# An adaptive layer-norm block on one core: the second batch's residual is stored ahead, and its gated tiles are added in the output by transfers from GpSimd

## The chip, the cores and the metric

One core of one Trainium2 chip runs the whole program. The metric is the device time of one execution in microseconds. A time given for a kernel is the median of several executions; a trace is one execution taken with the hardware profiler, and has its own time and its own span (from the first to the last recorded instruction).

## The reference

Two batches of 512 tokens with 512 features, all in float32. A condition vector `c` per batch gives six rows of modulation (shift, scale and gate for each of two sublayers).

```
mod = silu(c) @ wmod                      # per batch: sa, ca, ga, sb, cb, gb
ga, gb = sign * max(abs(.), 0.25)
h = layernorm(x) * (1 + ca) + sa
x = x + ga * (h @ (weight * blockmask).T)
h = layernorm(x) * (1 + cb) + sb
g = silu((h @ Wg.T) * ag) * ((h @ Wu.T) * au)      # 1376 inner features
out = x + gb * ((g @ Wd.T) * ad)
```

What matters here is the last line: the final result is the residual `x` after the first sublayer, plus a product that is scaled by a gate row per batch.

## The kernel before, in words

The tokens are held as eight tiles of 128 tokens by 512 features, `xt[:, n, :]`, four of each batch (`TT` is 4, `n = b * TT + t`). The kernel writes each engine's program out by hand, in one order, and ties the engines together with semaphores; there is no scheduler.

The first part loads the inputs, makes the modulation columns, normalises, and multiplies by the masked attention weight. GpSimd's `add_to_x` (L310) adds the gated product to `xt` and raises `x1_ok`: from then on `xt` holds the residual of the second sublayer, for `n` = 0 to 7. These tiles are normalised again (L497, for the second batch into `modw`), and for the second batch SyncE's sixteen block copies (L266) and VectorE's transposes (L504) bring them into the form that the matmuls want.

The feed-forward part runs over `STEPS` = 22 steps, 11 chunks of inner features for each batch. In a step TensorE makes the gate and up products (L793), ScalarE the silu, VectorE their product in two parts, and two steps later TensorE multiplies by the down weight into four accumulators, banks 4 to 7, one for each token tile (L863). For the second batch's last tile the accumulator is in two halves of 256 columns, in bank 7 and bank 3 (L849). `down_last` runs the last four steps' down products tile by tile, so that the accumulators are finished one after the other: tile 0, 1, 2, then the two halves of tile 3. `acc_mm` and `half_mm` say so.

Two rows of gates, one per batch, are broadcast over all partitions into `gates`: ScalarE copies them into `grow`, SyncE writes them to `gate_line` in memory (L270) and loads them back to all partitions (L273).

The end of a batch: VectorE's `gate_ffn(b, t)` (L619) multiplies an accumulator by the gate row, into `xn[:, t, :]`, and raises `acc_read`. For the first batch GpSimd adds it to `xt` (L329) and SyncE stores the tile (L278). For the second batch VectorE does both: after each `gate_ffn(1, t)` it waits for it and adds `xn` to `xt` (L685), then the same for the two halves of tile 3 (L691, L694). ScalarE's queue issues the stores of the second batch as `out_last` counts up, three whole tiles (L451) and two halves (L456). SyncE's last wait is for all nine stores.

SyncE's queue in order of its program: the loads, the sixteen block copies, the wait for `grow_ok`, the two writes of `gate_line`, the broadcast load, the four stores of the first batch, the last wait. GpSimd's queue: constants, `add_to_x`, the reciprocal deviations, and last the four additions of the first batch.

Of the kernel before, what the change touches and what calls it, by code (L numbers as in the profile page):

```python
# [25 lines left out]
ALU = mybir.AluOpType  # L26
# [3 lines left out]
P = 128  # L30
D = 512
KT = D // P
NB = 2
TT = 4
# [10 lines left out]
BY_POOL = TT  # L45
# [6 lines left out]
HALF = D // 2  # L52
# [14 lines left out]
def adaln_block(nc, x, att_w, att_mask, cond, mod_ln1, mod_ln2, mod_gate, w_gu, w_gu_tail, w_down,  # L67
                scales, scales_tail, down_scale, out):
    with ExitStack() as ctx:
# [3 lines left out]
        def sem(name):  # L73
            return ctx.enter_context(nc.semaphore(name))


        xt = sb("xt", [P, NB * TT, D])
        xn = sb("xn", [P, TT, D])
# [70 lines left out]
        d_ffn = [sem(f"d_ffn{c}") for c in range(C)]  # L149
        d_small = sem("d_small")  # L150
        d_out = sem("d_out")

        zeroed = sem("zeroed")
        tail_zero = sem("tail_zero")
# [36 lines left out]
        x1_ok = sem("x1_ok")  # L191
# [15 lines left out]
        acc_mm = sem("acc_mm")  # L207
        acc_read = sem("acc_read")
        out_ok = sem("out_ok")
        out_last = sem("out_last")  # L210
        half_mm = sem("half_mm")
        half_read = sem("half_read")

# [10 lines left out]
        @block.sync  # L224
        def _(sp):
            for t in range(TT):
                sp.dma_start(xt[:, t, :], x[t * P:(t + 1) * P, :]).then_inc(d_x[t], 16)  # L227

            def load_att(k):
                sp.dma_start(maskt[:, k, :], att_mask[k * P:(k + 1) * P, :]).then_inc(d_mask[k], 16)  # L230

                sp.dma_start(modw[:, k // 2, 2 * (k % 2):2 * (k % 2) + 2, :], mod_ln1[k])\
                  .then_inc(d_ln1[k], 16)
                sp.dma_start(awork[:, k, :], att_w[k * P:(k + 1) * P, :]).then_inc(d_att[k], 16)

            def load_x(t):
                sp.dma_start(xt[:, t, :], x[t * P:(t + 1) * P, :]).then_inc(d_x[t], 16)

            for k in range(KT):
                load_att(k)  # L240
            for t in range(TT, NB * TT):
                load_x(t)
            sp.dma_start(modw[:, 2, :, :], mod_gate[0]).then_inc(d_gate[0], 16)
            sp.wait_ge(rows_done, 2)
            sp.dma_start(modw[:, 0, :, :], mod_ln2[0]).then_inc(d_ln2[0], 16)
            for c in range(C):
                if c == H1_CHUNK:
                    sp.wait_ge(att_done, NB * TT)
                if c == 1:
                    sp.wait_ge(rows_done, 4)  # L250
                    sp.dma_start(modw[:, 1, :, :], mod_ln2[1]).then_inc(d_ln2[1], 16)
                    sp.wait_ge(rows_done, KT + 1)
                    sp.dma_start(modw[:, 2, :, :], mod_gate[1]).then_inc(d_gate[1], 16)
                if c < C - 1:
                    sp.dma_start(wffn[:, c, 0:2 * D], w_gu[c]).then_inc(d_ffn[c], 16)
                    sp.dma_start(raw_d(c), w_down[c * P:(c + 1) * P, :]).then_inc(d_ffn[c], 16)
                else:
                    sp.wait_ge(tail_zero, 1)
                    sp.dma_start(wffn[:, c, 0:2 * D].rearrange("p (n i) -> p n i", i=P)[:, :, 0:FT],
                                 w_gu_tail).then_inc(d_ffn[c], 16)  # L260
                    sp.dma_start(wffn[0:FT, c, 2 * D:3 * D], w_down[c * P:F, :])\
                      .then_inc(d_ffn[c], 16)
            sp.wait_ge(xn_ok, 4 * TT)
            for j in range(P // BLK):
                for i in range(P // BLK):
                    sp.dma_start(modw[BLK * j:BLK * (j + 1), 1, :, i * P:(i + 1) * P],  # L266
                                 modw[BLK * i:BLK * (i + 1), 0, :, j * P:(j + 1) * P]).then_inc(d_blocks[j], 16)
            sp.wait_ge(grow_ok, 1)
            for b in range(NB):
                sp.dma_start(gate_line[b], grow[b * KT:(b + 1) * KT, :]).then_inc(d_line, 16)  # L270
            sp.wait_ge(d_line, 16 * NB)
            sp.wait_ge(msum_ok, KT)
            sp.dma_start(gates[:, NB:2 * NB, :].rearrange("p b n -> p (b n)"),  # L273
                         gate_line.rearrange("b k i -> (b k i)").partition_broadcast(P))\
              .then_inc(d_gates, 16)
            for n in range(BY_POOL):
                sp.wait_ge(out_ok, n + 1)
                sp.dma_start(out[n * P:(n + 1) * P, :], xt[:, n, :]).then_inc(d_out, 16)  # L278
            sp.wait_ge(d_out, 16 * (NB * TT + 1))


        @block.gpsimd
        def _(pool):
            pool.memset(ident[:, :], 0.0).then_inc(ident_z, 1)
            pool.memset(mhalf[:, :], -0.5).then_inc(ident_z, 1)
            pool.wait_ge(ident_z, 2)
            pool.affine_select(out=ident[:, :], in_=ident[:, :], compare_op=ALU.not_equal, fill=1.0,  # L287
                               base=0, pattern=[[-1, P]], channel_multiplier=1).then_inc(ident_ok, 1)

            def inverse_deviation(q, half):  # L290

                two = slice(2 * half, 2 * half + 2)
                pool.wait_ge(stats_ok, TT * q + 2 * half + 2)
                pool.tensor_scalar(veps[:, q, two], mv[:, q, two, 1], EPS, None, ALU.add)\
                    .then_inc(veps_ok, 1)
                pool.wait_ge(veps_ok, 2 * q + half + 1)
                pool.tensor_tensor(rstd[:, q, two], veps[:, q, two], mhalf[:, 0:2], ALU.pow)\  # L297
                    .then_inc(rstd_ok, 1)

            def mask_weights(k):  # L300
                pool.wait_ge(d_att[k], 16)
                pool.wait_ge(keep_ok, k + 1)
                w = awork[:, k, :].rearrange("p (b i) -> p b i", i=BLK)
                pool.tensor_tensor(w, w, keep[:, k, :].unsqueeze(2).to_broadcast([P, NBLK, BLK]),
                                   ALU.mult).then_inc(masked, 1)

            def add_to_x(b, t):
                n = b * TT + t
                pool.wait_ge(att_read, n + 1)
                pool.tensor_tensor(xt[:, n, :], xt[:, n, :], xn[:, t, :], ALU.add).then_inc(x1_ok, 1)  # L310

            inverse_deviation(0, 0)
            inverse_deviation(0, 1)
            for k in range(KT):
                mask_weights(k)
            inverse_deviation(1, 0)
            inverse_deviation(1, 1)
            for b in range(NB):
                for t in range(TT):
                    add_to_x(b, t)  # L320
                inverse_deviation(2 + b, 0)
                inverse_deviation(2 + b, 1)
                if b == 0:

                    pool.wait_ge(att_done, NB * TT)
                    pool.memset(wffn[:, C - 1, :], 0.0).then_inc(tail_zero, 1)
            for n in range(BY_POOL):
                pool.wait_ge(acc_read, n + 1)
                pool.tensor_tensor(xt[:, n, :], xt[:, n, :], xn[:, n % TT, :], ALU.add)\  # L329
                    .then_inc(out_ok, 1)  # L330


        @block.scalar
        def _(act):
# [92 lines left out]
            for s in range(STEPS):  # L427
# [18 lines left out]
                    act.activation(grow[:, :], bank[3][0:KT * NB, 0:P], ACT.Copy).then_inc(grow_ok, 1)  # L446
                if 6 <= s < 10:
                    modulate(6 + s)
            for n in range(BY_POOL, NB * TT - 1):
                act.wait_ge(out_last, n - BY_POOL + 1)  # L450
                act.dma_start(out[n * P:(n + 1) * P, :], xt[:, n, :]).then_inc(d_out, 16)  # L451
            n = NB * TT - 1
            for i in range(2):
                cols = slice(i * HALF, (i + 1) * HALF)
                act.wait_ge(out_last, n - BY_POOL + 1 + i)
                act.dma_start(out[n * P:(n + 1) * P, cols], xt[:, n, cols]).then_inc(d_out, 16)  # L456


        @block.vector
        def _(dve):  # L460
# [218 lines left out]
                    for t in range(TT):  # L679
                        gate_ffn(0, t)  # L680
            for t in range(TT - 1):
                n = TT + t
                gate_ffn(1, t)
                dve.wait_ge(acc_read, n + 1)
                dve.tensor_tensor(xt[:, n, :], xt[:, n, :], xn[:, t, :], ALU.add)\  # L685
                   .then_inc(out_last, 1)
            n = NB * TT - 1
            for i, src in enumerate((bank[7], bank[3])):
                cols = slice(i * HALF, (i + 1) * HALF)
                dve.wait_ge(half_mm, i + 1)  # L690
                dve.scalar_tensor_tensor(xn[:, TT - 1, cols], src[:, cols], 2.0, gates[:, 3, cols],  # L691
                                         ALU.mult, ALU.mult).then_inc(half_read, 1)
                dve.wait_ge(half_read, i + 1)
                dve.tensor_tensor(xt[:, n, cols], xt[:, n, cols], xn[:, TT - 1, cols], ALU.add)\  # L694
                   .then_inc(out_last, 1)


        @block.tensor
# [363 lines left out]
```

## Time and profile before

| | us |
|---|---|
| median of 3 runs | 178.72 (178.65 to 178.88) |
| the profiled execution, its own time | 178.94 |
| its span | 176.7 |
| TensorE busy | 170.0 (96%) |
| VectorE busy | 96.6 (55%) |
| GpSimd busy | 30.0 (17%) |

The span is from the first to the last recorded instruction; the execution's own time is 2.24 us longer. The busy shares are means over the whole span. TensorE's granted clock was full throughout (0.999 on average). The transfer engines are 33.3% busy with SyncE's queue and 1.8% with ScalarE's, most of it in the first half. Times in rows are counted from the start of the span. In rows, "ACTq" and "SPq" are the queues from which ScalarE and SyncE issue transfers, and a line number is that of the kernel before.

### The profile page before, as it was taken

To read this page: it belongs to the slowest core of one execution; us is meant where nothing else is said; L and a number is where in the kernel's file an instruction comes from. 1 tells how busy PE (TensorE), PEld (TensorE's weight loads), DVE (VectorE), ACT (ScalarE), POOL (GpSimd) and SP (SyncE) were. 2 spreads that over 40 slices of the span, in tenths; PEclk is the share of its full clock that TensorE was granted. 3 is DMA by queue.
4 is the path that set the end of the run, shared out by engine and by line. 5 is a ranking of instruction groups with operands and counts; after the bars stand their busy time and mean duration, and the time that the engine had idled before them with its cause. 6 is when DMAs were issued, how large, how long until landed. Compare 5 with 4: busy or idle time off the path is not lost.

```text
span 176.7 us, 2566 instructions
## 1 busy us (share of the span) xinstructions
PE 170.0 (96%) x915; PEld 130.1 (74%) x915; DVE 96.6 (55%) x196; ACT 81.9 (46%) x115; POOL 30.0 (17%) x40
## 2 busy tenths in 40 slices
PE   6879999999999999999999999999999999999992
PEld 6745536666558888788888888888888888888882
DVE  6882662486574998335555664327644224442574
ACT  3032213787586987833665444543345433352200
POOL 1443420293009440000000000005600000000000
PEclk9999999999999999999999999999999999999999
DMA  5999998999308600431300000000500000000014
GB/s 165 362 409 395 421 408 328 396 410 400 115 6 281 212 4 15 104 93 31 122 0 4 6 0 0 4 0 32 209 4 0 4 0 4 0 6 0 4 59 178
DMA packets 11812, 22.93 MB, mean 130 GB/s; under 512 B 2728, under 2 KB 5040, under 8 KB 11280
## 3 DMA queue, kind: packets, MB, share of 16 engines
q1 hardware_dynamic: 10528, 21.57, 33.3%
q10 hardware_dynamic: 1264, 1.07, 1.8%
q8 instruction: 16, 0.26, 0.6%
q14 instruction: 4, 0.03, 0.1%
HBM read 19.48 MB, written 2.10 MB: 122 GB/s over the span
## 4 chain that ended last, share of the span: by engine, by line
PE 91%; DVE 4%; DMA 3%; SPq 1%; issue 0%
PE bank L793 45%; PE bank L863 20%; PE bank L763 16%; PE bank L707 3%; PE bank L747 3%; DMA xt<-in_x 3%; PE bank L849 2%; DVE xn L497 1%; SPq L227 1%; PE bank L771 0%; DVE xt L694 0%; DVE bns L478 0%; DVE xn L619 0%; DVE xn L691 0%; DVE xt L685 0%
## 5 line engine op out<-in xcount | busy, mean ns | idle before, releaser
L793 PE MATMUL bank<-ht,whi_gu 128*128 128x512 f32 x352 | 83.6, 391 | 0.0
L793 PEld LDWEIGHTS bank<-ht,whi_gu 128*128 128x128 f32 x352 | 65.6, 188 | 13.9 <-issue 0.5
L600 DVE SCALAR_TENSOR_TENSOR awork<-bank,scal,awork 128x512 f32<-128x512 f32 x22 | 16.5, 750 | 51.1 <-PE bank L793 48.6
L863 PE MATMUL bank<-whi_dn,in_split 128*128 128x512 f32 x148 | 37.1, 390 | 0.0
L438 ACT ACTIVATE awork<-bank,scal 128x512 f32<-128x512 f32 x22 | 15.2, 690 | 44.6 <-PE bank L793 44.5
L863 PEld LDWEIGHTS bank<-whi_dn,in_split 128*128 128x128 f32 x148 | 27.7, 188 | 5.8
L763 PE MATMUL bank<-awork,wffn 128*128 128x512 f32 x64 | 31.2, 605 | 0.0
L395 ACT ACTIVATE whi_gu<-wffn 128x1024 fp32r<-128x1024 f32 x22 | 23.3, 1058 | 7.3 <-PE bank L793 7.3
L609 DVE TENSOR_TENSOR in_split<-awork,in_split 128x512 fp32r<-128x512 f32 x21 | 16.5, 785 | 0.7
L763 PEld LDWEIGHTS bank<-awork,wffn 128*128 128x128 f32 x64 | 10.6, 190 | 8.1 <-issue 7.2
L388 ACT ACTIVATE junk<-wffn 128x1536 uint8<-128x1536 uint16 x11 | 16.3, 1479 | 0.4
L329 POOL TENSOR_TENSOR xt<-xt,xn 128x512 f32<-128x512 f32 x4 | 5.2, 1346 | 55.0 <-DVE xn L619 55.0
L403 ACT ACTIVATE whi_dn<-wffn 128x512 fp32r<-128x512 f32 x21 | 13.1, 623 | 0.0
L310 POOL TENSOR_TENSOR xt<-xt,xn 128x512 f32<-128x512 f32 x8 | 10.2, 1316 | 8.6 <-DVE xn L578 8.6
L478 DVE BATCH_NORM_STATS2 bns<-xt 128x6 f32<-128x512 f32 x16 | 10.9, 680 | 1.3 <-POOL xt L310 0.7
L376 ACT ACTIVATE wffn<-bank,modc 128x512 f32<-128x512 f32 x8 | 6.2, 776 | 9.7 <-DVE modc L533 6.1
L607 DVE CAST in_split<-awork 128x512 fp32r<-128x512 f32 x21 | 9.0, 430 | 0.7
L747 PEld LDWEIGHTS bank<-ident,xn 128*128 128x128 f32 x48 | 5.7, 141 | 5.0 <-issue 4.0
L747 PE MATMUL bank<-ident,xn 128*128 128x128 f32 x48 | 6.9, 274 | 0.8 <-DVE xn L497 0.8
L354 ACT ACTIVATE rows<-bank 128x128 f32<-128x128 f32 x6 | 1.7, 277 | 13.0 <-PE bank L707 13.0
L939 PE MATMUL bank<-ident 128*128 128x128 f32 x34 | 6.0, 359 | 1.5 <-POOL ident L287 1.5
L497 DVE TENSOR_SCALAR xn<-xt,mv,rstd 128x512 f32<-128x512 f32 x12 | 6.7, 603 | 1.0 <-POOL rstd L297 0.8
(67 smaller groups left out, 109.0 us busy)
## 6 DMA issues: line engine op xcount, KB each, us to landing
wffn<-in_w_gu SPq DMA_DIRECT2D x10, 512.0 KB, 8.1
wffn<-in_w_down SPq DMA_DIRECT2D x10, 256.0 KB, 9.1
xt<-in_x SPq DMA_DIRECT2D x8, 256.0 KB, 6.7
modw<-in_mod_ln SPq DMA_DIRECT2D x4, 512.0 KB, 7.1
modw<-in_mod_gate SPq DMA_DIRECT2D x2, 1024.0 KB, 8.3
modw<-in_mod_ln SPq DMA_DIRECT2D x2, 1024.0 KB, 11.3
maskt<-in_att_mask SPq DMA_DIRECT2D x4, 256.0 KB, 6.3
awork<-in_att_w SPq DMA_DIRECT2D x4, 256.0 KB, 7.1
```

The costliest lines, as they stand in the source:

```text
L310: pool.tensor_tensor(xt[:, n, :], xt[:, n, :], xn[:, t, :], ALU.add).then_inc(x1_ok, 1)
L388: act.activation(junk[:, :], low, ACT.Copy, accum_out=chk[:, c:c + 1])\
L395: act.activation(whi_gu[:, s % 2, :], wffn[:, s % C, 0:2 * D], ACT.Copy)\
L403: act.activation(whi_d(s), raw_d(s % C), ACT.Copy).then_inc(wd_hi, 1)
L438: act.activation(silu_g[:, s % 2, :], bank[gu_bank(s, 0)][:, :], ACT.Silu, scale=scal[:, s % C, 0:1]).then_inc(silu_ok, 1)
L478: dve.bn_stats(bns[:, q, t, :], xt[:, n % (NB * TT), :]).then_inc(bn_done, 1)
L600: dve.scalar_tensor_tensor(inner[:, s % 2, :], bank[gu_bank(s, 1)][:, :], scal[:, c, 1:2], silu_g[:, s % 2, :], ALU.mult, ALU.mult).then_i ...
L609: dve.tensor_tensor(lo, inner[:, s % 2, :], hi.bitcast(F32), ALU.subtract)\
L747: last = pe.transpose(dst[:, t * P:(t + 1) * P], xn[:, t, k * P:(k + 1) * P], ident[:, :])
L763: last = pe.matmul(bank[4 * b + t][:, :], h1[:, b, k, t * P:(t + 1) * P], awork[:, k, :], start=(k == 0), stop=(k == KT - 1))
L793: return pe.matmul(bank[gu_bank(s, u)][:, :], w, h, start=(k == 0 and part == 0), stop=(k == KT - 1 and part == 1))
L863: last = pe.matmul(bank[4 + t][:, :], h, w, start=(c == 0 and part == 0), stop=(c == C - 1 and part == 1))
```

## The change

- SyncE waits for all eight residual tiles and stores the second batch's four into the output, between the block copies and the wait for `grow_ok`. Each store has a semaphore of its own, `d_x1`.
- VectorE only gates: the additions of the second batch (L685, L694) and the semaphore `out_last` are gone. `gate_ffn(1, t)` for the three whole tiles and the gating of the two halves remain as they were.
- ScalarE issues no stores.
- GpSimd, after its four additions of the first batch, issues five transfers from `xn` to the output with an accumulate operation (add): three of whole tiles, 256 KB each, and two of half tiles, 128 KB each. Each waits for its tile's first store and for the gating, and GpSimd waits for all five at the end. SyncE's last wait is for the first batch's four stores.

```diff
@@ sync
+            sp.wait_ge(x1_ok, NB * TT)
+            for t in range(TT):
+                n = TT + t
+                sp.dma_start(out[n * P:(n + 1) * P, :], xt[:, n, :]).then_inc(d_x1[t], 16)
             sp.wait_ge(grow_ok, 1)
...
-            sp.wait_ge(d_out, 16 * (NB * TT + 1))
+            sp.wait_ge(d_out, 16 * TT)
@@ gpsimd
+            for t in range(TT - 1):
+                n = TT + t
+                pool.wait_ge(d_x1[t], 16)
+                pool.wait_ge(acc_read, n + 1)
+                pool.dma_start(out[n * P:(n + 1) * P, :], xn[:, t, :], accum_op=ALU.add).then_inc(d_add[t], 16)
+            n = NB * TT - 1
+            pool.wait_ge(d_x1[TT - 1], 16)
+            for i in range(2):
+                cols = slice(i * HALF, (i + 1) * HALF)
+                pool.wait_ge(half_read, i + 1)
+                pool.dma_start(out[n * P:(n + 1) * P, cols], xn[:, TT - 1, cols], accum_op=ALU.add)\
+                    .then_inc(d_add[TT - 1 + i], 16)
+            for done in d_add:
+                pool.wait_ge(done, 16)
@@ scalar
-            for n in range(BY_POOL, NB * TT - 1):
-                act.wait_ge(out_last, n - BY_POOL + 1)
-                act.dma_start(out[n * P:(n + 1) * P, :], xt[:, n, :]).then_inc(d_out, 16)
-            n = NB * TT - 1
-            for i in range(2):
-                cols = slice(i * HALF, (i + 1) * HALF)
-                act.wait_ge(out_last, n - BY_POOL + 1 + i)
-                act.dma_start(out[n * P:(n + 1) * P, cols], xt[:, n, cols]).then_inc(d_out, 16)
@@ vector
                 gate_ffn(1, t)
-                dve.wait_ge(acc_read, n + 1)
-                dve.tensor_tensor(xt[:, n, :], xt[:, n, :], xn[:, t, :], ALU.add)\
-                   .then_inc(out_last, 1)
...
-                dve.wait_ge(half_read, i + 1)
-                dve.tensor_tensor(xt[:, n, cols], xt[:, n, cols], xn[:, TT - 1, cols], ALU.add)\
-                   .then_inc(out_last, 1)
```

## Rows read from the trace of the kernel before

**Rows 1.** The page: busy time and share, and the chain by engine.

```profile
PE 170.0 (96%) x915; PEld 130.1 (74%) x915; DVE 96.6 (55%) x196; ACT 81.9 (46%) x115; POOL 30.0 (17%) x40
...
PE 91%; DVE 4%; DMA 3%; SPq 1%; issue 0%
```

**Rows 2.** The chain that ended last, from 165 us: start, duration, what.

```profile
166.00 5.55 PE bank L863 x24
...
171.57 0.70 DVE xn L619
...
173.36 0.43 DVE xt L694
173.79 0.34 DVE xn L691
...
174.15 0.42 DVE xt L694
```

**Rows 3.** The timeline of TensorE from 167.9 us: start, duration, instructions.

```profile
168.10 0.67 PE L863 MATMUL bank<-ht 128*128 128x512 f32 x2
...
169.07 0.62 PE L863 MATMUL bank<-ht 128*128 128x512 f32 x2
...
170.92 0.62 PE L863 MATMUL bank<-ht 128*128 128x512 f32 x2
...
172.09 0.40 PE L849 MATMUL bank<-ht 128*128 128x256 f32 x2
...
173.04 0.40 PE L849 MATMUL bank<-ht 128*128 128x256 f32 x2
```

**Rows 4.** Transfers by tensor: count, size of one, median us from issue to landing.

```profile
modw<-modw SPq DMA_DIRECT2D x16, 64.0 KB, 2.0
...
out<-xt ACTq DMA_DIRECT2D x3, 256.0 KB, 2.1
maskt<-gate_line SPq DMA_DIRECT2D x1, 512.0 KB, 3.8
...
out<-xt ACTq DMA_DIRECT2D x2, 128.0 KB, 1.7
...
condt<-in_cond ACTq DMA_DIRECT2D x1, 4.0 KB, 3.0
```

**Rows 5.** The timeline of ScalarE's queue from 174.5 us.

```profile
174.61 0.34 ACTq L456 DMA_DIRECT2D out<-xt  x1
```

**Rows 6.** The timeline of VectorE from 169 us.

```profile
168.81 0.69 DVE L619 SCALAR_TENSOR_TENSOR xn<-bank,maskt 128x512 f32<-128x512 f32 x1 [0.83 <-PE bank L863]
169.54 0.69 DVE L685 TENSOR_TENSOR xt<-xt,xn 128x512 f32<-128x512 f32 x1
...
172.91 0.42 DVE L691 SCALAR_TENSOR_TENSOR xn<-bank,maskt 128x256 f32<-128x256 f32 x1
```

**Rows 7.** The timeline of SyncE's queue from 60 us.

```profile
68.71 10.92 SPq L266 DMA_DIRECT2D modw<-modw  x16
82.54 0.60 SPq L270 DMA_DIRECT2D gate_line<-grow  x2
84.06 0.35 SPq L273 DMA_DIRECT2D maskt<-gate_line  x1
```

**Rows 8.** Waits of SyncE's queue: total us, times, longest.

```profile
SPq L270 <- ACT grow L446: 2.9, 1, 2.9
```

**Rows 9.** Stretches: busy time by engine, then clock, transfer share, GB/s.

```profile
80.00:82.00 2.00, 2.00 (x12) 1.55 (x10) 1.60 (x3) 0.00 (x0) 0.00 (x0) 1.00 0.15 35
...
174.00:174.60 0.60, 0.00 (x0) 0.00 (x0) 0.54 (x2) 0.00 (x0) 0.00 (x0) 1.00 0.96 358
```

**Rows 10.** The timelines of VectorE and GpSimd from 119.5 us.

```profile
120.42 2.48 DVE L619 SCALAR_TENSOR_TENSOR xn<-bank,maskt 128x512 f32<-128x512 f32 x4
...
121.18 5.23 POOL L329 TENSOR_TENSOR xt<-xt,xn 128x512 f32<-128x512 f32 x4 [55.01 <-DVE xn L619]
```

**Rows 11.** Queues of transfers: packets, MB, share of 16 engines' span.

```profile
q1 hardware_dynamic: 10528, 21.57, 33.3%
q10 hardware_dynamic: 1264, 1.07, 1.8%
```

More of the change, by code:

```diff
@@ L151, in adaln_block @@
         d_out = sem("d_out")
+        d_x1 = [sem(f"d_x1_{t}") for t in range(TT)]
+        d_add = [sem(f"d_add{n}") for n in range(TT + 1)]
         zeroed = sem("zeroed")
@@ L209, in adaln_block @@
         out_ok = sem("out_ok")
-        out_last = sem("out_last")
         half_mm = sem("half_mm")
@@ L681, in _ @@
             for t in range(TT - 1):
-                n = TT + t
                 gate_ffn(1, t)
-                dve.wait_ge(acc_read, n + 1)
-                dve.tensor_tensor(xt[:, n, :], xt[:, n, :], xn[:, t, :], ALU.add)\
-                   .then_inc(out_last, 1)
-            n = NB * TT - 1
             for i, src in enumerate((bank[7], bank[3])):
```

## The prediction

> **What bounds the kernel now.** I read the page's busy shares first: TensorE is busy for 96% of the span, and the chain that ended last lies 91% on it [rows 1]. Nothing in the diff touches a matmul, so the body of the kernel can't get shorter. What the change can move is what follows the last matmul, and what it puts in the middle. So the second view is the chain of waits in its last stretch [rows 2]: TensorE until 171.55, and from then on VectorE alone, each operation right behind the one before. The third is TensorE's timeline there [rows 3]. It gives the end of each accumulator: 168.77 (tile 0 of the second batch), 169.69 (tile 1), 171.54 (tile 2), 172.49 (first half of tile 3), 173.44 (second half). VectorE's last addition ends at 174.15 + 0.42 = 174.57, that is 1.13 us behind the last matmul. The fourth view is the issues and landings of transfers [rows 4, 5]: the last half is issued by ScalarE's queue at 174.61 and a store of 128 KB lands 1.7 us from its issue, at 176.31. The span ends at 176.7, 0.39 us later. So the tail is 3.26 us: 0.45 of gating of the last half (with the wait for VectorE to be free), then 0.42 of addition, 0.34 of issue, 1.4 of transfer and receipt, and the rest of closing. That VectorE is late is seen too: the last gating starts at 173.79 in the chain, and its matmuls were done at 173.44.
>
> **What is removed.** Three additions of a whole tile (0.69 each) and two of a half (0.42 each) go from VectorE [rows 2, 6]. With them gone each gating can start when its matmuls end. Behind TensorE's ends, with 0.03 us between engines (171.54 to 171.57 in rows 2 and 3) and 0.69 or 0.42 per gating, the gated tiles are ready at: tile 0 169.50, tile 1 170.41, tile 2 172.26, first half 172.94, second half 173.89. The last data to be sent is thus ready 0.68 us sooner than before (174.57). ScalarE's five issues go as well; nothing stood behind them on its queue.
>
> **What is added in the middle.** SP's queue gets one wait and four stores of 256 KB, between the sixteen block copies and the wait for `grow`. The wait on `x1_ok` costs nothing: the block copies themselves wait for the normalised tiles, which were made from those very sums. The copies end at 68.71 + 10.92 = 79.63 and SP then waits 2.9 us for `grow` [rows 7, 8]. Four issues of 0.34 (as the last store on ScalarE's queue [rows 5]) are 1.4 us and fit into it. Their 1 MB takes some 2.9 us at the 358 GB/s that the stores reach when they fill the engines, in a stretch where these are 15% busy [rows 9]; so until about 83. The two small writes of `grow` at 82.54 and the broadcast behind them come up to 1 us later, the broadcast to land near 88.9 where it was 84.06 + 3.8 = 87.9 [rows 4, 7]. Its first reader is the gating of the first batch at 120.42 [rows 10]. Cost nothing; the cover is 31 us. Without it a microsecond would go straight to the accumulators' release. The block copies, which VectorE's transposes wait for, are issued ahead of the stores and are not held. The stores land long before the first accumulating transfer needs them at 169.5.
>
> **What is added at the end.** GpSimd issues five transfers that read the output, add and write it. Its queue is empty: its last work was the four additions of the first batch, 121.18 to 126.41 [rows 10]. None of the trace's transfers is issued by GpSimd, and none adds: q1 and q10, SP's and ScalarE's, are hardware queues and carry them all [rows 11]. So both terms have to be bounded.
>
> Term G, GpSimd's time per issue. Low end: 0.34, what SP and ScalarE take [rows 5]. High end: 1.31, GpSimd's own pass over a 128x512 tile (5.23 / 4) [rows 10]. The row of like work is between them: the block copies, of 32 partitions in four pieces each, cost SP 0.68 apiece (10.92 / 16) [rows 7]. I take the middle of these two, the row of like work and the row of this engine: 1.0, for a whole tile and for a half alike, since both have 128 rows.
>
> Term L, from the end of the issue to the landing. Low end: 1.36, a plain store of 128 KB (1.7 less 0.34) [rows 4, 5]. High end: the store and a whole small read of memory, one after the other: 1.36 + (3.0 - 0.34) = 4.0, by the 4 KB load of `condt` [rows 4]. Between: the broadcast's read lands 3.8 from its issue; less 0.35 of issue and 1.46 of moving 512 KB at 358 GB/s, 2.0 is latency; a copy within SBUF has 2.0 - 0.6 = 1.4. Reading memory rather than SBUF so costs 0.6 more, and a second stream of 128 KB another 0.37 at that rate: L = 1.36 + 0.97 = 2.33, which I take.
>
> The queue, with G = 1.0: tile 0 from 169.50 to 170.50, tile 1 to 171.50, tile 2 from 172.26 to 173.26, first half (ready 172.94) to 174.26, second half (ready 173.89) to 175.26. Landing 175.26 + 2.33 = 177.59, against 176.31 before: 1.28 us later. What the last step gives up: of the 1.37 us by which the last issue ends behind its data, 1.0 is its own and 0.37 is waiting behind its neighbours. The queue begins to bind when G is over (173.89 - 172.26) / 2 = 0.82. The waits for the five semaphores cost nothing beside the last landing, and I leave the 0.39 of closing as it is.
>
> Sum: the profiled execution's own time is 178.94 (span 176.7, 2.24 around it). 178.94 + 1.28 = 180.22 in a like execution. The median of the runs is 178.72, 0.22 below that one, so **180.0**.
>
> The Trainium skill bears on this sum in one place ("DMA: Bandwidth & Descriptors"). Its section "Anatomy of one DMA — SWDGE (gpsimd) path" has a fit for a transfer issued from GpSimd, 2.0 us plus the bytes at 436 GB/s. By it 128 KB land 2.3 us behind the trigger, at 176.2, which would be no change. The same page ("Latency and other measured facts") puts the first byte at about 1 us for GpSimd and 0.6 for the hardware queues; 0.4 us over the plain store would have the last half land at 176.0. The trace agrees with it for the hardware queues as far as size goes (128 KB in 1.7, 256 KB in 2.1), and has no row for GpSimd's. Neither figure is for a transfer that adds or for five in a row. So I rank it as the rival of no change.
>
> **Rivals.**
> Rival 1, the transfer is cheap and the change is faster. The point from which it decides is G + L = 176.31 - 173.89 = 2.42, with G under 0.82. At both low ends, 0.34 + 1.36, the landing is at 175.59, 0.72 sooner: 178.0. For it: VectorE really sits between the matmuls and the last issue, with 0.68 us to win, and a plain 128 KB needs only 1.7. Against it: it needs an issue as fast as hardware's and nothing for reading memory first; the trace's loads all take longer than its stores.
> Rival 2, the two cancel. G = 0.6 (near the block copies' price) does not queue; with L = 1.36 + 0.4, an adding read that hides partly under the transfer, the last half lands at 173.89 + 2.36 = 176.25: 178.7, no change.
> Rival 3, GpSimd's queue is the new tail. G = 1.31: tile 2 to 173.57, the halves to 174.88 and 176.19; L = 4.0 gives 180.19, 3.9 us later: 182.6. Splitting tile 3 then harms, since it buys a second issue in a row. For it: GpSimd takes 1.31 for a pass over a tile that VectorE makes in 0.69, and whatever it does per transfer could be as slow; a first transfer of this kind is in no row at all. Against it: both high ends at once.
> Rival 4, the stores in the middle hold up something on SP's queue. Against it are the 2.9 us of idle wait and the 31 us of cover; a loss would show at 120 as a late gating, some 0.5 us: 179.2.
>
> **How the numbers follow.** The forecast's own case (0.4 to 2.5 us later) 0.55; rival 1 0.10; rival 2 0.13; rival 3, from 2.5 us upward, 0.20; rival 4 0.02. A measurement of this kernel tells a difference over about 0.2%, 0.36 us. Slower is 0.55 + 0.20 + 0.02 = 0.77, the same 0.13, faster 0.10. The range leaves out most of rival 1 and the far end of rival 3: 178.4 to 182.4.
>
> **What would show it.** The middle: SP's issues of 256 KB near 80, the wait for `grow` shorter by 1.4 us, first gating still at 120.4, last matmul still at 173.4. VectorE: gatings at about 168.8, 169.7, 171.6, 172.5 and 173.5, nothing behind them. GpSimd: five issues near 1 us each, the last ending at about 175.3, and the last landing over 2 us behind it. I am wrong if the issues are short (under 0.5 us) and the landing under 2 us, which is rival 1; if each issue is over 1.2 us or the landing over 3.5 us, it is rival 3; if the last matmul has moved by more than 0.3 us, the change reached into the body in a way that I have not seen.

## The result, and the profile after

The changed kernel is slower: 182.57 us (182.29 to 183.30, 4 runs) against 178.77, a ratio of 1.02 with a 95% interval of 1.0154 to 1.0246. A second set of runs, later and beside other kernels, gave 181.95 (181.18 to 182.48) and a ratio of 1.0181 (1.0124 to 1.0238). The direction was the forecast's, the size was not: 3.8 us more instead of 1.3, just past the range's upper end of 182.4 (the second set's 181.95 lies inside it). The profiled execution took 182.29, its span was 180.2.

The busy shares of the page after show that the body is as it was. TensorE and ScalarE have the same busy time, VectorE lost its five additions, and GpSimd gained five instructions and 4.7 us. The second line is the chain's shares, in which GpSimd now stands at the end.

```profile
PE 170.1 (94%) x915; PEld 130.3 (72%) x915; DVE 93.9 (52%) x191; ACT 81.9 (45%) x115; POOL 34.7 (19%) x45
...
PE 89%; DMA 3%; DVE 2%; POOL 1%; issue 1%; SPq 1%; POOLq 0%
```

The timelines from 168 us (start, duration, instruction, and in brackets the idle time before) answer to [rows 3, 6]. Gatings follow their matmuls at once, as in the prediction; GpSimd's issues are instructions of its own, and the last of them ends at 173.58 + 1.94 = 175.52.

```profile
168.90 0.69 DVE L630 SCALAR_TENSOR_TENSOR xn<-bank,maskt 128x512 f32<-128x512 f32 x1 [0.82 <-PE bank L866]
...
170.24 1.99 POOL L340 DMA_DIRECT2D out<-xn  x2 [43.72 <-DVE xn L630]
...
172.89 0.86 POOL L340 DMA_DIRECT2D out<-xn  x1 [0.66 <-DVE xn L630]
...
173.13 0.40 PE L852 MATMUL bank<-ht 128*128 128x256 f32 x2
173.56 0.42 DVE L697 SCALAR_TENSOR_TENSOR xn<-bank,maskt 128x256 f32<-128x256 f32 x1 [0.53 <-PE bank L852]
173.58 1.94 POOL L346 DMA_DIRECT2D out<-xn  x2
```

The transfers, by tensor, answer to [rows 4]: the adding ones land 5.0 us from the start of their issue, where plain ones of the same sizes took 2.1 and 1.7.

```profile
out<-xn POOLq DMA_DIRECT2D x3, 256.0 KB, 5.0
...
out<-xn POOLq DMA_DIRECT2D x2, 128.0 KB, 5.0
```

And the same stretch by windows (engines' busy time, clock, share of the transfer engines, GB/s). This is the view that I had not thought of in advance. From the first adding packet to the last it is 7.2 us, in which 1.05 MB are moved. The share is 0.99 on average, but it is uneven (0.38 from 172.0 to 172.5, 0.65 from 174.0 to 174.5) and goes over 1.0, so it is a rough measure. At their steadiest, with every issue over, the engines make 180 GB/s. Before, they stored at 358 in a full window [rows 9].

```profile
171.50:178.70 7.20, 2.03 (x17) 1.82 (x15) 1.54 (x3) 0.00 (x0) 3.36 (x4) 0.87 0.99 145
176.00:178.00 2.00, 0.00 (x0) 0.00 (x0) 0.00 (x0) 0.00 (x0) 0.00 (x0) 0.69 1.13 180
```

**Where the 3.5 us of span come from.** The last matmul ends at 173.53, 0.09 later than before. I call the time from there to the span's end the tail: 3.26 before (173.44 to 176.7), 6.67 after (173.53 to 180.2). All but that 0.09 of the difference is in it. The body moves by a microsecond or more from one execution to the next, and the tail does not: a second profiled execution of the changed kernel had its last matmul at 172.46 and its span end at 179.1, a tail of 6.64. So the experiments are read by their tails first, and by the medians as a check.

### The profile page after: what moved, and what is told of

Same layout as the page of the kernel before. It is cut to its first block, busy times and chain, and to the rows that moved or that the text cites. A ratio compares the mean times of both kernels' runs of the same rounds, so it can differ in the third digit from the quotient of the medians.

```text
span 180.2 us, 2572 instructions
## 1 busy us (share of the span) xinstructions
PE 170.1 (94%) x915; PEld 130.3 (72%) x915; DVE 93.9 (52%) x191; ACT 81.9 (45%) x115; POOL 34.7 (19%) x45
## 3 DMA queue, kind: packets, MB, share of 16 engines
q0 software_dynamic: 720, 1.05, 3.9%
## 4 chain that ended last, share of the span: by engine, by line
PE 89%; DMA 3%; DVE 2%; POOL 1%; issue 1%; SPq 1%; POOLq 0%
PE bank L796 44%; PE bank L866 20%; PE bank L766 16%; PE bank L710 3%; PE bank L750 3%; DMA xt<-in_x 3%; PE bank L852 2%; DVE xn L508 1%; POOL out L346 1%; SPq L228 1%; PE bank L774 0%; DVE bns L489 0%; DVE xn L630 0%; DVE msum L520 0%; PE bank L724 0%
## 5 line engine op out<-in xcount | busy, mean ns | idle before, releaser
L340 POOL DMA_DIRECT2D out<-xn x3 | 2.8, 1032 | 44.4 <-DVE xn L630 44.4
```

## The experiments

Each was run in 3 rounds beside the kernel before. Tails are worked out as above, from the end of TensorE's last row to the end of the span.

| kernel | tail | time, median | ratio to before (95%) |
|---|---|---|---|
| before | 3.26 | 178.77 to 178.86 | |
| the changed kernel | 6.67 | 182.57 | 1.02 (1.0154 to 1.0246) |
| the same again | 6.64 | 181.95 | 1.0181 (1.0124 to 1.0238) |
| plain GpSimd stores | 3.86 | 179.64 | 1.0037 (0.9997 to 1.0078) |
| no additions, ScalarE stores | 2.61 | 178.19 | 0.9958 (0.9923 to 0.9993) |
| only the halves add | 5.85 | 181.52 | 1.0134 (1.0083 to 1.0185) |
| only the middle stores | 3.26 | 178.80 | 0.9973 (0.9936 to 1.0009) |
| half the bytes | 4.68 | 180.00 | 1.0105 (1.0042 to 1.0167) |
| SyncE waits | 6.59 | 183.37 | 1.0222 (1.0158 to 1.0287) |
| last tile in one transfer | 6.77 | 181.74 | 1.0163 (1.0136 to 1.019) |
| GpSimd adds tile 2 itself | 3.45 | 179.15 | 1.0019 (0.9983 to 1.0055) |
| middle stores by GpSimd | 3.53 | 179.31 | 1.0012 (0.9975 to 1.0048) |
| tile 2 alone adds | 4.65 | 179.89 | 1.008 (1.0045 to 1.0114) |

### Is it the adding, or GpSimd's path?

```diff
-                pool.dma_start(out[n * P:(n + 1) * P, :], xn[:, t, :], accum_op=ALU.add).then_inc(d_add[t], 16)
+                pool.dma_start(out[n * P:(n + 1) * P, :], xn[:, t, :]).then_inc(d_add[t], 16)
...
-                pool.dma_start(out[n * P:(n + 1) * P, cols], xn[:, TT - 1, cols], accum_op=ALU.add)\
+                pool.dma_start(out[n * P:(n + 1) * P, cols], xn[:, TT - 1, cols])\
...
```

> The changed kernel with its five GpSimd transfers made plain stores of the gated tiles (no add; the residual of the second batch is so left out of the output). Theory T: a transfer that adds holds the engines about 2.5 times as long per row as a plain one, so five of them back up (the engines are 99% busy from 171.5 to 178.7 in the trace after) and the last lands when the backlog is gone. Plain stores then leave no backlog: the last issue ends at 175.5, lands 1.4 to 1.6 later, and with 0.9 of closing the span is about 178, the time about 180.1. Rival S: GpSimd's issuing path is slow in itself, adding or not, and the landing 5 us from the issue stays: 182 to 182.6.

Measured: 179.64, tail 3.86. Theory T holds in the main (it had said 180.1), rival S falls. The first issue takes 0.77 and the other four 0.54 or 0.55, half of an adding one (0.86 to 1.24); the halves land 2.1 and the whole tiles 2.5 from its start. GpSimd's timeline of the two halves:

```profile
173.50 0.54 POOL L346 DMA_DIRECT2D out<-xn  x1
174.20 0.54 POOL L346 DMA_DIRECT2D out<-xn  x1 [0.16 <-issue]
```

The chain of the same kernel (start, duration, what) shows a cost that no busy row has: 0.5 us between GpSimd's queue seeing the semaphore (POOLq) and the issue that is recorded.

```profile
172.29 0.02 POOLq L339
172.31 0.51 issue
172.82 0.18 POOL out L340
```

### What is taking the additions from VectorE worth?

```diff
-                act.wait_ge(out_last, n - BY_POOL + 1 + i)
-                act.dma_start(out[n * P:(n + 1) * P, cols], xt[:, n, cols]).then_inc(d_out, 16)
+                act.wait_ge(half_read, i + 1)
+                act.dma_start(out[n * P:(n + 1) * P, cols], xn[:, TT - 1, cols]).then_inc(d_out, 16)
...
-                dve.tensor_tensor(xt[:, n, cols], xt[:, n, cols], xn[:, TT - 1, cols], ALU.add)\
-                   .then_inc(out_last, 1)
```

(The whole tiles likewise.)

> The kernel before without VectorE's additions of the second batch, ScalarE's queue storing the gated tiles as they are (the residual of the second batch is left out). It measures what taking the additions from VectorE is worth by itself. My step says the last half is ready 0.68 us sooner, so 178.05. If VectorE's additions were not on the path: 178.7.

Measured: 178.19, tail 2.61. That is 0.65 less than before, and the step said 0.68. The last gating starts at 173.42, its matmuls having ended at 173.39.

```profile
173.42 0.42 DVE xn L687
```

These two kernels and the changed one split the 3.41 us into three: taking away VectorE's additions gives back 0.65, GpSimd's queue in place of ScalarE's costs 3.86 - 2.61 = 1.25, and adding instead of storing costs 6.67 - 3.86 = 2.81. Of the 2.81, 0.7 are the longer issues (the last one ends 1.99 behind the last matmul instead of 1.30), and the rest comes after the last issue.

### Backlog, or a latency of each adding transfer?

```diff
+            for t in [TT - 1]:
+                n = TT + t
+                sp.dma_start(out[n * P:(n + 1) * P, :], xt[:, n, :]).then_inc(d_x1[t], 16)
...
+                pool.wait_ge(half_read, i + 1)
+                pool.dma_start(out[n * P:(n + 1) * P, cols], xn[:, TT - 1, cols], accum_op=ALU.add)\
+                    .then_inc(d_add[TT - 1 + i], 16)
```

(The three whole tiles as in the kernel before.)

> The kernel before, with only the last tile's two halves accumulated by GpSimd onto a residual stored ahead; the three whole tiles as before. Theory T (backlog): 8 rows per engine at 0.18 us are 1.44 us for a half, no queue in front of it, so the last half lands about 1.9 us from the end of its issue at 175.4: span 178.2, time about 180.4. Rival R (a fixed latency of the adding transfer, whatever is in front of it): it lands 3.9 us from the end of its issue as after, and the time stays at 182.3.

Measured: 181.52, tail 5.85, between the two. With no adding tile in front of them the halves land 3.3 and 3.8 us from the start of their issues (median 3.6) instead of 5.0. The transfers of this kernel (count, size, us to landing), and the end of its chain (start, duration, what):

```profile
out<-xn POOLq DMA_DIRECT2D x2, 128.0 KB, 3.6
```

```profile
174.98 0.44 DVE xn L701
...
175.48 1.99 POOL out L342 x2
```

The tails differ by only 6.67 - 5.85 = 0.82, but that understates the backlog, since in this kernel the last issue comes later: it ends at 177.47, 2.52 behind the last matmul, where it ended 1.99 behind it in the changed kernel. VectorE still adds the three whole tiles here, so the first half's gating ends 0.12 before the last matmul does instead of 0.49, and GpSimd's first issue starts 0.65 behind the gating. From the end of the last issue to the landing it is 3.8 us in the changed kernel, 2.6 here (176.27 + 3.8 - 177.47) and 1.6 with plain stores. So the tiles in front account for 1.2 of the 2.2 us by which an adding half lands later than a plain one, and adding the halves alone for 1.0. Theory T had the direction, but put the landing at 1.9 and the issue's end 0.5 too early; rival R's 3.9 falls. (This profiled execution took 182.82 and its last matmul ended at 174.95; its tail is free of that.)

### By rows or by bytes?

```diff
-                pool.dma_start(out[n * P:(n + 1) * P, :], xn[:, t, :], accum_op=ALU.add).then_inc(d_add[t], 16)
+                pool.dma_start(out[n * P:(n + 1) * P, 0:HALF], xn[:, t, 0:HALF], accum_op=ALU.add).then_inc(d_add[t], 16)
...
-                pool.dma_start(out[n * P:(n + 1) * P, cols], xn[:, TT - 1, cols], accum_op=ALU.add)\
+                part = slice(i * HALF, i * HALF + HALF // 2)
+                pool.dma_start(out[n * P:(n + 1) * P, part], xn[:, TT - 1, part], accum_op=ALU.add)\
```

> The changed kernel with every adding transfer cut to half of its columns: the same 640 rows, half the bytes (the other half of the second batch's output keeps the bare residual). So far: the tail behind the last matmul is 3.26 us before, 6.67 after, 3.86 with plain GpSimd stores, 5.85 with the two halves alone adding. From these traces a row of 1 KB that is added takes an engine 0.16 us and one of 2 KB 0.19. Theory P (a price per row, little by bytes): 40 rows per engine at 0.15 to 0.16 are 6.2 us instead of 7.2, the tail 5.6 to 6.0, the time about 181.7. Rival B (a price by bytes): the backlog halves, no queue is left, tail about 4.5, time 180.3.

```diff
-            for i in range(2):
-                cols = slice(i * HALF, (i + 1) * HALF)
-                pool.wait_ge(half_read, i + 1)
-                pool.dma_start(out[n * P:(n + 1) * P, cols], xn[:, TT - 1, cols], accum_op=ALU.add)\
-                    .then_inc(d_add[TT - 1 + i], 16)
+            pool.wait_ge(half_read, 2)
+            pool.dma_start(out[n * P:(n + 1) * P, :], xn[:, TT - 1, :], accum_op=ALU.add).then_inc(d_add[TT - 1], 16)
```

> The changed kernel with the last tile added by one transfer of 128 rows of 2 KB behind its second half, instead of two transfers of 128 rows of 1 KB. Theory P (price per row): 32 rows per engine instead of 40, 6.1 us instead of 7.2, so the tail is about 5.7 and the time 181.5: faster than two halves. Rival B (by bytes): the same backlog with the last part started later, tail 6.7 or more, 182.5 or more.

Measured: half the bytes on as many rows take the tail to 4.68, next to rival B's 4.5. A fifth fewer rows with the same bytes leave it at 6.77, where rival B had 6.7 or more and theory P 5.7. (This kernel's median, 181.74, lay under rival B's 182.5, and its ratio of 1.0163 is no different from the changed kernel's 1.0181 in its second set.) Theory P, a price per row and little by bytes, falls. The 0.16 and 0.19 us that I had read per row came from busy shares, which go over 1.0 in these windows (1.13 above), so they are no durations.

A price by bytes alone is not shown either. The windows behind the last issue, of the kernel with half the bytes (rows of 512 B by then), of the one with one last transfer (rows of 2 KB) and of the one where only the halves add (rows of 1 KB):

```profile
174.90:176.30 1.40, 0.00 (x0) 0.00 (x0) 0.00 (x0) 0.00 (x0) 0.00 (x0) 1.00 0.95 90
```

```profile
175.40:178.50 3.10, 0.00 (x0) 0.00 (x0) 0.00 (x0) 0.00 (x0) 0.00 (x0) 0.91 1.13 188
```

```profile
177.50:179.50 2.00, 0.00 (x0) 0.00 (x0) 0.00 (x0) 0.00 (x0) 0.00 (x0) 0.78 0.96 114
```

The engines are as good as full in all three, and they move 90, 188 and 114 GB/s. So the same bytes don't always cost the same, and with half the bytes the stretch from the first adding packet to the last is 5.4 us, not half of 7.2 (4.0 of it pass before the last issue is over, at 174.9). Short rows may be a part of it. They are not all of it: in the changed kernel's window from 176.00 to 178.00, at 180 GB/s, three quarters of the rows are of 1 KB too. As for one transfer in place of two, the engines move 188 GB/s behind its issue where the changed kernel moved 163 (175.5 to 178.5), but it is issued 0.24 later than the second half was, and from 174.0 to 175.4 the engines are 79% busy with 97 GB/s. How the price splits between bytes, rows and the depth of the backlog, and what in an adding transfer costs the time (reading, adding or writing), no run here separates.

### The middle, the closing, and who waits

```diff
+            for t in range(TT):
+                n = TT + t
+                sp.dma_start(out[n * P:(n + 1) * P, :], xt[:, n, :]).then_inc(d_x1[t], 16)
             sp.wait_ge(grow_ok, 1)
...
```

> The kernel before with only the four stores in the middle added (the final stores overwrite them, after waiting for them). Predicted as free: 178.7. Rival: the stores hold up SyncE's queue or the transfer engines for something that is on the path: 179.0 or more.

Measured: 178.80, tail 3.26. Free, as predicted.

```diff
+            for done in d_add:
+                sp.wait_ge(done, 16)
...
-            for done in d_add:
-                pool.wait_ge(done, 16)
```

> The changed kernel with the last five waits moved from GpSimd to SyncE, nothing else. The closing, from the last landing to the span's end, was 0.4 us where SyncE waited (before, and with no additions) and 0.9 to 1.0 where GpSimd did (after, and with plain GpSimd stores). If GpSimd's waiting is what costs: 0.5 less, tail 6.2, time 182.0. If it is the software queue itself (its landing is reported later to whoever waits): no change, tail 6.7, 182.5.

Measured: tail 6.59, and 4.60 from the last issue's end to the span's end where it was 4.68. The 0.5 us that would have come back did not. The median, 183.37, is above both expectations, with a ratio of 1.0222 beside the changed kernel's 1.02. (This profiled execution took 185.75 and its last matmul ended at 177.21; only the stretch behind that is compared here, and it is one trace.)

```diff
+            for t in range(TT):
+                n = TT + t
+                pool.dma_start(out[n * P:(n + 1) * P, :], xt[:, n, :]).then_inc(d_x1[t], 16)
             for n in range(BY_POOL):
...
+            for t in range(TT):
+                dve.wait_ge(d_x1[t], 16)
             for t in range(TT - 1):
```

> The kernel before, with the four stores in the middle added and issued by GpSimd as plain stores (the final stores overwrite them); nothing at the end goes over GpSimd. It asks where the 0.5 us of longer closing come from that every kernel with GpSimd transfers has (0.9 to 1.0 from the last landing to the span's end instead of 0.4), whoever waits for them. If a program that has used GpSimd's queue at all pays it: tail behind the last matmul 3.26 + 0.5 = 3.8, time about 179.3. If only a last transfer on that queue pays it: tail 3.26, time 178.8.

Measured: 179.31, tail 3.53, between the two. The median alone would speak for the first (179.3), but its ratio of 1.0012 (0.9975 to 1.0048) can't tell them apart. The trace can: from VectorE's last addition (174.04 + 0.42) to the span's end it is 2.14, against 2.13 before. So using GpSimd's queue earlier costs nothing at the end; the 0.5 us go with a last transfer on that queue. The other 0.27 of this tail is VectorE standing later behind TensorE. It begins at its first gating, which starts 0.41 behind its matmuls (168.81 against 168.40) where it was 0.04 before, and in front of this gating the edit puts four waits of VectorE for the early stores. That these waits cost it is likely and not shown: no run has them alone.

### Is there a version that wins?

```diff
+            n = NB * TT - 2
+            pool.wait_ge(acc_read, n + 1)
+            pool.tensor_tensor(xt[:, n, :], xt[:, n, :], xn[:, TT - 2, :], ALU.add).then_inc(out_ok, 1)
...
```

(VectorE's addition of tile 2 is gone, and SyncE stores this tile.)

> A version against both: the kernel before, but tile 2's addition is GpSimd's own pass (as it does for the first batch) and SyncE stores the tile; nothing accumulates in memory. If the passes run side by side: last addition ends at 174.34 instead of 174.57, tail 3.0, time 178.5. Rival: GpSimd's pass and VectorE's addition of two tiles in SBUF hold each other up (in the trace of before one such subtraction took 1.67 us instead of 0.69 beside GpSimd's additions): the first half's addition waits for GpSimd until about 173.6, the last one ends at about 174.9, tail 3.6, time 179.1.

Measured: 179.15, tail 3.45. The rival holds in its mechanism: the first half's addition takes 0.93 instead of 0.42 while GpSimd's pass runs until 173.64, and the second gating starts late for it. The last addition ends at 174.71, between the 174.34 and the rival's 174.9. VectorE's timeline:

```profile
172.99 0.93 DVE L701 TENSOR_TENSOR xt<-xt,xn 128x256 f32<-128x256 f32 x1
173.84 0.41 DVE L698 SCALAR_TENSOR_TENSOR xn<-bank,maskt 128x256 f32<-128x256 f32 x1
```

and GpSimd's timeline of the same kernel:

```profile
172.35 1.29 POOL L336 TENSOR_TENSOR xt<-xt,xn 128x512 f32<-128x512 f32 x1 [45.92 <-DVE xn L625]
```

```diff
+            n = NB * TT - 2
+            pool.wait_ge(d_x1[TT - 2], 16)
+            pool.wait_ge(acc_read, n + 1)
+            pool.dma_start(out[n * P:(n + 1) * P, :], xn[:, TT - 2, :], accum_op=ALU.add).then_inc(d_add[0], 16)
...
```

(In the middle only tile 2's residual is stored, VectorE's addition of tile 2 is gone, and SyncE waits for the adding transfer.)

> The kernel before, but tile 2 of the second batch alone is added in the output by a GpSimd transfer; tiles 0, 1 and 3 are added on VectorE and stored over ScalarE's queue. VectorE's last addition then ends at 174.34 instead of 174.57. The transfer is issued until 173.7, is the only one that adds, and drains 256 KB at 100 to 180 GB/s: it lands at 176.2 to 177.0, behind the last plain store at 176.1. With 0.9 of closing the tail is 3.7 to 4.4, the time 179.2 to 179.9: slower than before. Rival: with a single adding transfer its cost hides behind the halves: tail 3.1, time 178.5.

Measured: 179.89, tail 4.65, even a little worse than expected. VectorE's last addition ends at 174.37, as said, and gains nothing: a single adding transfer of 256 KB lands 4.5 us from its issue, and the plain halves beside it take 2.5 instead of 1.7.

```profile
out<-xn POOLq DMA_DIRECT2D x1, 256.0 KB, 4.5
out<-xt ACTq DMA_DIRECT2D x2, 128.0 KB, 2.5
```

The last run was the changed kernel once more, for the tail's spread.

> The changed kernel unchanged, a second profiled execution beside runs of the kernel before: the tail behind the last matmul again 6.6 to 6.7 us, the time 182.3 to 182.6. A tail that moved by over 0.3 us would say that the comparisons of tails between single traces are looser than I take them to be.

Measured: tail 6.64, 181.95. The tail is as steady as I took it to be; the median came 0.35 under the expectation, and in the profiled execution the last matmul ended 1.07 sooner. No kernel here that computes the whole output beats the one before. One that adds only the earliest tiles by transfers was not run.

## Why the prediction was right and where it was wrong

**What bounds, and the gain.** Right. The gatings began at 168.90, 169.82, 171.66, 172.61 and 173.56 (predicted 168.8, 169.7, 171.6, 172.5, 173.5, with TensorE 0.09 later), and the last data were ready 0.6 us sooner. The kernel without additions shows 0.65 in its tail. The list of what makes up the 3.26 us of the tail had one reading wrong: the last gating starts at 173.70 in VectorE's timeline (the chain shows only its last 0.34), and from the last matmul to the start of the last addition it is 0.71, not 0.45. With 0.71 the list adds up to 3.26, and the 0.68 did not use it.

**The middle.** Right. The block copies end at 79.84, the four stores take 2.08 in issues instead of 1.4, the wait for `grow` is 0.7 instead of 2.9, and the first batch's gating starts at 120.52. The middle alone costs nothing that the runs can show (tail 3.26, ratio 0.9973 with 0.9936 to 1.0009).

```profile
79.89 2.08 SPq L272 DMA_DIRECT2D out<-xt  x4
82.64 0.62 SPq L275 DMA_DIRECT2D gate_line<-grow  x2
```

**Term G, GpSimd's issue.** About right: 0.86 to 1.24 us where I took 1.0. The last issue ended at 175.52, predicted 175.26. But it is made up otherwise than I thought: 0.5 us or a little more pass before an issue that found the queue empty, and an issue that adds takes about twice as long as a plain one (0.54). The fear of rival 3, that GpSimd's queue would be the tail, did not come true; the last half's issue ended 1.54 us behind its data (173.98), of which 0.31 was waiting (I had said 0.37) and 1.23 its own (I had said 1.0).

**Term L, from the issue's end to the landing, is the step that failed.** I took 2.33, and the last half's was 174.29 + 5.0 - 175.52 = 3.8. I had built it as a latency: a plain store, plus 0.6 for reading memory, plus 0.37 for a second stream at the rate of the first. The runs put a rate and a backlog in its place. With the engines full, adding moves 90 to 188 GB/s where plain stores move 358. So the five transfers are a megabyte that takes 7.2 us from 171.5, longer than the 4.4 us in which the data arrive (169.59 to 173.98). Plain stores by the same queue landed 1.6 behind the issue's end (2.1 - 0.54). Of the 2.2 more, the tiles in front account for 1.2 and the halves' own adding for 1.0, by the kernel in which only the halves add. My bounds held it (1.36 to 4.0), and I chose the wrong place within them: I had priced one transfer, at the rate of a plain one, and not asked how fast the sum of the five drains. By the prediction's own sign (a landing over 3.5) this is rival 3's case. (The 0.6 for reading memory has a small slip too: a block copy's issue is 0.68 by the rows, not 0.6. It changes L by 0.08.)

**The closing was left as it is, 0.39, and was 0.9.** It is longer whenever the last transfer to land is on GpSimd's queue: 0.7 to 1.0 in eight traces, against 0.4 with ScalarE's. Where SyncE waits for it instead of GpSimd it is 0.8 and 0.7, within that range, and an earlier use of the queue adds nothing. What the extra time is, no run here shows.

**The sum of the misses:** 1.4 for L, 0.5 for the closing, 0.3 for the last issue's end; together 2.2, and with the forecast's 1.28 that is the 3.5 by which the span grew. Rival 3 had nearly the right time, 182.6, and that was in part luck: a landing near its L of 4.0 was there, but from a backlog and a slower rate, not from a store and a read one after the other, and its G of 1.31 and the long queue on GpSimd were not there. The prediction also took a measurement to tell 0.2% apart; the intervals here are about 0.4% to either side.

**The Trainium skill's fit** ("DMA: Bandwidth & Descriptors", section "Anatomy of one DMA — SWDGE (gpsimd) path": 2.0 us plus the bytes at 436 GB/s) gives 2.3 for 128 KB. For GpSimd's plain stores the trace comes near, 2.1 from the start of the issue, plus some 0.5 ahead of it where the queue was empty. For adding transfers the measurement decides, and for 128 KB it is 3.3 to 3.8 with no tile in front and 5.0 with three.

## What to carry to other kernels

A transfer that adds in memory is not a plain store with an addition for free. Price it by a rate, measured on transfers like its own, sum the bytes of all that come within a few microseconds, and compare the drain with what is left of the kernel: here 1 MB needed 7.2 us, and the VectorE work that it replaced was worth 0.65. It would belong where nothing waits for it; no run here tried that. And when the question is one of tails, compare them from the last matmul on: that number repeated within 0.03 us in two traces of one kernel whose spans differed by 1.1.

## What the runs showed that I had not expected

- Between a semaphore's arrival at GpSimd's queue and the recorded issue 0.5 us pass, in the chains of the changed kernel, of the one with plain stores and of the one with a single last transfer.
- An issue that adds occupies GpSimd for 0.86 to 1.24 us, one that stores mostly for 0.54 (0.77 for the first).
- With the engines about full, adding moves 188 GB/s in rows of 2 KB and 90 in rows of 512 B; in rows of 1 KB it was 114 in one kernel, and 180 in another with some 2 KB rows among them.
- Plain stores beside a transfer that adds took longer: 128 KB in 2.5 us instead of 1.7.
- A GpSimd addition of a tile stretched VectorE's addition of half a tile from 0.42 to 0.93 us, while VectorE's gating of the same half, which reads one operand from an accumulator, kept its 0.42 beside the same pass.
